# Moving the start-up work and the first two batches' fill-in layers in a one-core attention and feed-forward block

## The reference

```
xn  = layernorm(x)
att = attention(xn), 8 heads of width 128, rotary q and k, causal softmax, then the output projection wo
ffn = s2 * relu(s1 * relu(s0 * [xn, -xn] @ sign(k0)) * 2 @ sign(k1)) * 2 @ sign(k2)
out = x + att + ffn
```

## Time and profile before

| | |
|---|---|
| median of 3 executions | 1793.99 us (1793.79 to 1794.27) |
| the profiled execution's own time | 1793.79 us |
| its span | 1791.7 us |
| PE busy | 1760.3 us, 98% |
| DVE busy | 1450.5 us, 81% |
| ACT busy | 1093.7 us, 61% |
| POOL busy | 1042.3 us, 58% |
| granted clock of PE, mean | 0.996 |

### The profile page before, as it was taken

One profiled execution on the slowest core, in us unless ns is written; L12 is line 12 of the kernel. 1 busy time (PEld: TensorE's weight loads), 2 busy tenths in 40 slices (PEclk: granted clock), 3 DMA queues, 4 the chain that ended last, 5 costly groups with the idle time before them and its releaser, 6 DMA issues.

```text
span 1791.7 us, 30396 instructions
## 1 busy us (share of the span) xinstructions
PE 1760.3 (98%) x11280; PEld 1058.3 (59%) x11280; DVE 1450.5 (81%) x3275; ACT 1093.7 (61%) x2340; POOL 1042.3 (58%) x1065
## 2 busy tenths in 40 slices
PE   7899999999999999999999999999999999999999
PEld 3355556565665656656566565656656556565666
DVE  8898996878878788787887878888797887878865
ACT  4667665665656656565665656566566565666653
POOL 3567665655656555555655655556556555655652
PEclk9999999999999999999999999999999999999999
DMA  5233443343443343443434343343333333434333
GB/s 172 46 60 65 95 82 78 65 77 65 71 77 75 67 83 63 76 75 64 88 62 77 66 83 77 60 83 71 78 65 77 74 63 77 83 60 83 71 65 66
DMA packets 454820, 133.84 MB, mean 75 GB/s; under 512 B 434704, under 2 KB 453648, under 8 KB 454672
## 3 DMA queue, kind: packets, MB, share of 16 engines
q1 hardware_dynamic: 454672, 131.90, 38.3%
HBM read 14.94 MB, written 8.39 MB: 13 GB/s over the span
## 4 chain that ended last, share of the span: by engine, by line
PE 90%; DVE 6%; ACT 2%; DMA 1%; POOL 1%; SPq 0%; issue 0%; DVEq 0%; POOLq 0%
PE bank L385 90%; DVE ph L585 1%; ACT p L562 1%; DVE p L548 1%; DVE ta L502 1%; DVE qk L518 0%; DVE h L427 0%; DVE v L430 0%; DVE nm L556 0%; DVE xT L254 0%; DMA o<-in_k 0%; DVE p L260 0%; DMA xnat<-in_x 0%; DVE o L430 0%; DMA pt<-ph 0%
## 5 line engine op out<-in xcount | busy, mean ns | idle before, releaser
L579 POOL TENSOR_SCALAR ph<-p,ri 128x512 f16<-128x512 f32 (+3 forms) x512 | 341.3, 667 | 308.7 <-DVE rk L569 273.8
L506 POOL TENSOR_TENSOR tb<-tb,sin 128x512 f32<-128x512 f32 x256 | 329.2, 1286 | 293.4 <-ACT tb L496 290.2
L385 PE MATMUL bank<-h,w 128*128 128x512 f16 x2048 | 462.7, 379 | 0.0
L508 POOL TENSOR_TENSOR ta<-ta,tb 128x512 f32<-128x512 f32 x256 | 343.7, 1342 | 71.3 <-DVE ta L502 55.3
L562 ACT ACTIVATE p<-p,nm,sc 128x512 f32<-128x512 f32 (+3 forms) x512 | 327.5, 641 | 42.0 <-DVE nm L556 41.7
L495 ACT ACTIVATE tb<-bank 64x512 f32<-64x512 f32 x256 | 152.2, 594 | 289.4 <-PE bank L385 278.5
L385 PEld LDWEIGHTS bank<-h,w 128*128 128x128 f16 x2048 | 199.0, 98 | 216.9
L585 DVE SCALAR_TENSOR_TENSOR ph<-p,rk,ph 128x512 f16<-128x512 f32 (+3 forms) x512 | 314.0, 653 | 5.1 <-POOL ph L579 5.1
L514 ACT ACTIVATE qk<-ta 128x512 f16<-128x512 f32 x256 | 160.1, 625 | 176.9 <-POOL ta L508 176.9
L502 DVE TENSOR_TENSOR ta<-bank,cos 128x512 f32<-128x512 f32 x256 | 175.3, 685 | 84.2 <-ACT tb L496 84.0
L385 PE MATMUL bank<-qk 128*128 128x512 f16 (+3 forms) x1536 | 231.7, 301 | 9.8 <-DVE qk L518 9.8
(11 more groups left out here) (82 smaller groups left out, 1716.1 us busy)
## 6 DMA issues: line engine op xcount, KB each, us to landing
out<-xnat SPq DMA_DIRECT2D x32, 256.0 KB, 2.4
xnat<-in_x SPq DMA_DIRECT2D x15, 512.0 KB, 4.0
pt<-ph SPq DMA_TRANSPOSE x256, 4.3
o<-in_k SPq DMA_DIRECT2D x1, 1024.0 KB, 7.7
v<-in_wq SPq DMA_DIRECT2D x1, 1024.0 KB, 9.7
v<-in_wk SPq DMA_DIRECT2D x1, 1024.0 KB, 11.4
ph<-in_wv SPq DMA_DIRECT2D x1, 1024.0 KB, 13.6
o<-in_wo SPq DMA_DIRECT2D x1, 1024.0 KB, 10.8
```

The costliest lines, as they stand in the source:

```text
L385: self.todo.append(lambda e: e.matmul(self.ps[:, cols[0]:cols[1]], lhsT, rhs, start=start, stop=stop))
L506: a = pool.put(lambda e: e.tensor_tensor(tb, tb, SIN[:], ALU.mult))
L508: done["rot", n] = pool.put(lambda e: e.tensor_tensor(ta, ta, tb, ALU.add))
L579: done["P_hi", g, i] = pool.put(lambda e: e.tensor_scalar(part(r, i, HI), v, RI[:, g % 4, i:i + 1], 4096.0, ALU.mult, ALU.mult))
```

## The change

`AM` and `ONES` move to the buffer of `XT[:, 1]`, and the wait of the first two heads' `maxes` for `("KN", 2)` goes. `normal(1)` moves from ahead of the loop to the end of g = -1. The weight splits move: part 1 of q and k from g = -1 to g = -2, parts 2 and 3 from the end of g = -1 to its beginning, v from the end of g = -1 to the end of g = -2, the first half of wo from g = 0 to g = 2. The two `largest` of v and wo go on DVE's queue at once, ahead of the jobs of g = -2, and `turn_largest(2)` comes ahead of the last third of these jobs. The slots of `layer1` of batches 0 and 1 and of `layer2` of batch 0 change: layer1(0, 5) to (0, 7) from 0, 1, 1 to -1, -1, 0; layer1(1, 0) to (1, 7) from 5, 5, 6, 7, 7, 11, 12, 13 to 4, 5, 6, 7, 8, 9, 10, 11; layer2(0, 0) and (0, 1) from 2 and 4 to 1 and 2.

```diff
-        AM = P[:, 1, 0:256].rearrange("p (i n) -> p i n", i=2)
-        ONES = P[:, 1, 256:384]
+        AM = XT[:, 1].rearrange("p s t c n -> p (s t c n)").bitcast(F32)[:, 0:256].rearrange("p (i n) -> p i n", i=2)
+        ONES = XT[:, 1].rearrange("p s t c n -> p (s t c n)").bitcast(F32)[:, 256:384]
...
                     if g >= 2:
                         dve.wait(need(("P_lo", g - 2, 0)))
-                    else:
-                        dve.wait(need(("KN", 2)))
...
-                    slot = (-2, -2, -2, -2, -1, 0, 1, 1)[n]
+                    slot = (-2, -2, -2, -2, -1, -1, -1, 0)[n]
                 elif b == 1:
-                    slot = (-3, -3, -2, -1, -1, 3, 4, 5)[n]
+                    slot = (-4, -3, -2, -1, 0, 1, 2, 3)[n]
...
-                add_filler(z + (7 if last else 6 + k if b else 2 + 2 * k), 5, lambda b=b, k=k: layer2(b, k))
+                add_filler(z + (7 if last else 6 + k if b else 1 + k), 5, lambda b=b, k=k: layer2(b, k))
...
-        normal(1)
         for g in range(-2, G + 2):
...
-            if g == -1:
-                powers(2, 2.0 ** -30)
             if g == -2:
-                convert_k2()
-                at(3.5, lambda: largest(2, "v"))
-                at(9, lambda: largest(3, "o"))
-            if g == -1:
                 split_w("q", 0, 1, 4)
                 split_w("k", 1, 1, 4)
-            if g == 0:
-                at(30, lambda: split_w("o", 3, 0, 2))
+                convert_k2()
+                largest(2, "v")
+                largest(3, "o")
+            if g == -1:
+                for p in (2, 3):
+                    split_w("q", 0, p, 4)
+                    split_w("k", 1, p, 4)
             if g == 2:
-                split_w("o", 3, 1, 2)
+                for p in range(2):
+                    split_w("o", 3, p, 2)
...
+            if g == -2:
+                turn_largest(2)
             for job in third[2]:
                 job()
                 run_due()
             if g == -2:
-                turn_largest(2)
-            if g == -1:
-                for p in (2, 3):
-                    split_w("q", 0, p, 4)
-                    split_w("k", 1, p, 4)
+                powers(2, 2.0 ** -30)
                 for p in range(2):
                     split_w("v", 2, p, 2)
                 pads()
+            if g == -1:
+                normal(1)
```

## The result

| | before | changed |
|---|---|---|
| median | 1794.13 us (1793.79 to 1794.76, 4 runs) | 1809.38 us (1808.54 to 1810.19, 4 runs) |
| ratio | | 1.0085, 95% interval 1.0067 to 1.0102 |
| span of the profiled execution | 1791.7 us | 1808.0 us |

The change costs 15 us. The forecast was 1797.0 us, with a range from 1791 to 1802: slower, as that number said, but by 15 us and not by 3, and outside the range.

A forecast was written before the change was run, and what follows sets the result against it. PE, busy 98% of the span, was taken as the bound, with DVE bounding groups short of fillers. 1793.79 - 5.1 (gained by group 11) + 8.1 (lost in groups 12 to 14) = 1796.8, plus 0.2: 1797.0 us, range 1791 to 1802.

The forecast's parts named there:

- Part 1, the start: Up to layer2(0, 0)'s end at 81.6 us: scores(1)'s 6.53 us wait goes, PE leads by 8.6 us, DVE by 1.8.
- PE's lead at 214 units: At layer2(0, 0)'s end: 214 units of PE work (0.217 us each) done at 81.6 us against 90.2, 8.6 us ahead.
- Part 2, groups 2 to 5: DVE takes back part of PE's lead; scores(6) comes at 126.5 us with 395 units done instead of 379.
- The advantage at equal work is 4.7 us: At scores(6): 127.75 + 3.5 - 126.5 us, the gain left of PE's 8.6 us lead.
- DVE's lead: At the end of the start, DVE was claimed to be 1.8 us ahead of before, which set scores(6) at 126.5 us.
- (d): Rival, groups 2 to 5: clock falls after several waits; three slow stretches at 1.2 to 1.7 us make 1801; chance 0.10.
- Part 3, groups 5 to 11: PE and DVE level in groups 5 to 7, PE the bound in 8 to 11; 5.1 us gained by group 11's end.
- 0.5 us of waits: Groups 5 to 7: PE's 29.3 us against DVE's 30.2 called level, waits taken as 0.5 us, bounds 0 and 2.
- Rival (c): 43-unit groups 5 and 7 starve, waits of 2 us, one long enough for the slow clock: 1800 us; chance 0.19.
- Part 4, the hole: Groups 12 to 14, with 12 and 13 nearly or quite without fillers: waits of 7.0 and 4.1 us, loss 8.1 us.
- the term mis-sized: Slow clock after the waits before scores(14) and scores(15), taken as 2.3 and 1.7 us.

The follow-up runs named there:

- the repeated matmuls: Changed kernel with layer0(1, 2) and layer0(1, 3) matmuls done three times, values(1) twice, in group 2's short waits: 1806.35 us, ratio 1.007.
- normal(1) early: Changed kernel with normal(1) ahead of the loop again, AM and ONES in P, and the wait for KN: 1806.55 us, ratio 1.0071.
- the two runs with wo put back: Changed kernel with only the wo splits put back, 1807.03 us; with wo put back and batch 1 at 4, 5, 6, 7, 7, 11, 12, 13, 1799.05 us.
- the front-end run: Changed kernel with all slots and the splits of wo put back as before: 1793.45 us, ratio 0.9997.
- the batch 0 run: Changed kernel with wo put back and batch 1's layer1 at 4, 5, 6, 7, 7, 11, 12, 13: 1799.05 us, ratio 1.0025.
- the kernel before with the hole alone: Kernel before with layer1(1, 4) to (1, 7) moved from groups 7, 11, 12, 13 to 8, 9, 10, 11: 1802.17 us, ratio 1.0043.
- the busy-wait run: Changed kernel with 24 unread matmuls ahead of scores(14)'s wait and 12 ahead of scores(15)'s: 1804.04 us, ratio 1.0057.

## Why the prediction was wrong, point by point

**Part 1, the start.** Followed, the queue orders were right: the low part of k of head 0 was done at 50.2 against 48.2 + 1.3 (the later qk(0)), scores(0) didn't wait, scores(1) neither. But DVE's durations were mostly taken from rows where it ran undisturbed, and here it shared the time with POOL from the low part of k on. The changed kernel's timeline of DVE:

```profile
50.79 1.77 DVE L300 SCALAR_TENSOR_TENSOR wk<-v,kn,wk 128x512 f16<-128x512 f32 x1
...
59.56 0.69 DVE L518 TENSOR_TENSOR qk<-ta,qk 128x512 f16<-128x512 f32 x1 [1.22 <-ACT qk L514]
...
69.45 3.35 DVE L254 TENSOR_SCALAR xT<-xnat,mv,rs 128x256 f32<-128x256 f32 x4
72.72 0.68 DVE L502 TENSOR_TENSOR ta<-bank,cos 128x512 f32<-128x512 f32 x1
...
79.03 1.88 DVE L430 SCALAR_TENSOR_TENSOR v<-bank,v 128x512 f16<-128x512 f32 x3
...
91.07 3.49 DVE L300 SCALAR_TENSOR_TENSOR wo<-o,kn,wo 128x1024 f16<-128x1024 f32 x2 [0.93 <-ACT wo L298]
```

One wk split took 1.77 us where its neighbours took 0.7, norm_apply 3.35 (I had taken 3.1, with bounds; the 1.37 us row that I read as beside POOL half of the time is the time alone: in the kernel before, POOL was idle from 216.71 to 218.77 us), the wo halves 3.49 where two alone take 2.5. Up to the last v part that makes 1.3 us. DVE also stood idle for ACT, 1.22 us before 59.56 and 1.86 us before 62.11, which my following doesn't mention. And `straight` at 72.72 stood behind norm_apply(1) in DVE's queue, so that PE's v part at 73.46 waited 2.38 us for its bank, a wait that the forecast hadn't. The last v part ended at 80.9, that is 51.2 us after qk(0) and not 48.1; before it was 49.9. DVE did not lead by 1.8 us, it trailed by 1.3. PE's lead at 214 units came out as 4.0 us (5.3 from its own qk(0)) in the place of 8.6.

**Part 2, groups 2 to 5: the step that failed.** "The advantage at equal work is 4.7 us" became a loss of 3.1. It rested on DVE's lead, and on a rival set aside: (d), that the clock falls after several waits of 2 us at most. Two things happened. First, the lead was given back in waits for DVE. When layer2 of group 2 starts, 72.2 us after qk(0), the changed kernel has 16 units more done than the kernel before has at 68.7 us: 3.5 us later for 3.5 us of work, level at equal work. With the same fillers this date hardly moves, whatever else is edited: 72.3 with the repeated matmuls, 72.7 with normal(1) early, 72.7 and 73.1 in the two runs with wo put back. Then the clock fell: layer2(0, 1) took 6.25 us instead of 3.66, which is the whole 2.6 us by which group 3 is late, and the run with the repeated matmuls shows that its price can be had back (2.5 us). Which of DVE's items hold its date (the wo halves, the longer operations beside POOL, or PE's own lateness after a slow clock in groups 0 and 1) I can't part: each edit that took one away met another. That stays open. What the front-end run and the batch 0 run do settle is that bringing 32 units forward wins nothing at the end of group 2 and loses 2.7 us there. By the forecast's own reckoning, the 7.8 us by which scores(6) missed its place at equal work are 1.3 for the late qk(0), 3.1 for DVE's date at the last v part, 2.6 for the clock in layer2(0, 1), and 0.8 that I can't place.

The rule of the Trainium skill that I weighed and set aside ("TensorE: Matmul & The Clock Gate", "A second HAM failure mode: psum-queue depth-cycling") agrees with this trace: after waits of 0.48, 1.63, 1.51 and 2.09 us, 32 matmuls took 6.25 us and not 3.66, at a granted clock of 0.56.

**Part 3, groups 5 to 11.** I allowed 0.5 us of waits for two groups of 43 units. Scores(7) waited 1.33 us, scores(8) 0.46, values(6) 0.79, scores(10) 0.69. Of the wait for a transpose, which I had as gone, 0.79 us were still there, in group 7. Rival (c) had the place right, at least for group 5: with group 5 at 43 units the batch 0 run too waited 1.34 us for scores(7), while with group 7 alone at 43 units, in the kernel before with the hole alone, no wait followed. From scores(6) to the start of group 12 the difference grew by 3.0 us, where I had it fall by 0.4.

**Part 4, the hole.** The mechanism was right, and so were its waits: 7.46 and 3.99 us against 7.0 and 4.1. The order of the queues is as followed. Before, the low part of k (L518, at 222.67) ran ahead of the next head's `straight`; in the changed kernel two swap copies stand ahead of its high part on ACT, and both `straight` ahead of it on DVE:

```profile
233.02 0.59 ACT L496 ACTIVATE tb<-bank 64x512 f32<-64x512 f32 x1
233.63 0.63 ACT L514 ACTIVATE qk<-ta 128x512 f16<-128x512 f32 x1
...
235.96 0.68 DVE L502 TENSOR_TENSOR ta<-bank,cos 128x512 f32<-128x512 f32 x1
236.56 1.14 DVE L518 TENSOR_TENSOR qk<-ta,qk 128x512 f16<-128x512 f32 x1
```

No run put the old order back in the thin groups, so what the order alone costs is not shown; scores(14) came 17.4 us after the start of group 12, with 45 units of work before it, and before the change after 16.1 us with 61. The loss was 8.1 us in the forecast and is 10.2. Of the 2.1 us more, 0.7 is scores(14)'s own date (17.4 against 16.7). The rest is the clock, the term mis-sized: I took 2.3 + 1.7 us, measured it is 2.9 + 2.4, and the busy-wait run gives back 5.2. Scores(14) and scores(15) took 3.36 us each, values(12) 3.14 and the two layer0 behind scores(15) 2.77 instead of 1.89.

**Do the parts add up?** Front end -0.6 us (ratio 0.9997), fillers of batch 0 4.5 - (-0.6) = 5.1, the hole 7.7, wo 0.4 to 2.5: 12.6 to 14.7 us, against 15.2. The parts account for the change within their intervals. The 2.5 are, by the profile, rather the clock in group 14 than wo. Against the forecast, which is 13.3 us short at group 15, part 1 is off by 4.6 us (1.3 of them the late qk(0)), part 2 by 3.2, part 3 by 3.4 and part 4 by 2.1.

## What to carry to other kernels

An engine that is 98% busy may still be led by another one in every stretch that is short of its work: count, group by group, the second engine's time against the first one's, and move fillers only from groups with a reserve. Work brought forward wins only if the date at which it is handed over moves too; here DVE's date at the end of group 2 was no earlier at equal work, and the lead was given back in waits. A queue ordered by another engine's clock can change its order when that engine has less to do: follow it again for each thin group. In following a queue, take durations from rows in the same company (here: with POOL at work), count the waits for the engine in front as well, and give an idle PE its slower clock as a term of its own, with a range (here 2.7 to 5.2 us), wherever it is PE that the next step waits for.

## What the runs showed of the hardware

The clock does not go by the length of the last wait. The clearest pair are the stretches from scores(15) on, in the changed kernel and in the one with wo put back. Both come after a wait of 4.0 us, and before it the same matmuls at full clock and, further back, a wait of 7.5 us. The figure after the five engines is the granted clock, first of the changed kernel, then of the other, which got through 42 matmuls where the first did 21:

```profile
252.45:258.22 5.77, 5.77 (x21) 2.67 (x22) 3.67 (x12) 0.60 (x1) 4.38 (x6) 0.57 0.01 3
```

```profile
252.38:258.22 5.84, 5.84 (x42) 3.72 (x43) 4.96 (x14) 2.88 (x7) 4.95 (x6) 1.00 0.01 3
```

Short waits show the same. In the changed kernel waits of 2.38 and 1.63 us in groups 0 and 1 left the clock at 2.4 GHz (1.47 us for six matmuls). In the run with only batch 0's fillers nearly the same waits did not:

```profile
74.57 1.94 PE L385 MATMUL bank<-wv,xT 128*128 128x512 f16 x6 [2.37 <-DVE ta L502]
...
77.67 2.74 PE L385 MATMUL bank<-xT,wq 128*128 128x512 f16 x6 [1.16 <-DVE h L427]
```

What decides between the two is not shown here. And a slow clock may cost all or nothing: up to 5.2 us in the thin groups, where the chain ran through PE, and nothing measurable in the kernel before, where DVE was late behind the same kind of wait.
